# A hand-written order of work: its table of shifts and stretches with other numbers

## The reference

```
layer 0: qkvo = 1x1 conv(x); lepe = depthwise 5x5 conv(v)        # 12 heads of 32
         out  = proj((softmax(q k^T) v + lepe) * o)
layer 1: four directions k of a selective scan over 1024 points, 16 states n:
         dt = softplus(w_dt x_dbl + bias); h = exp(dt A) h + (dt u) B;  y += h C
         then layernorm over channels and gelu
layer 2: every group of channels shifted, then a 5x5 blur (here two small matmuls)
layer 3: softmax attention over 1024 points (one head), squeeze-and-excite gate, proj, batchnorm
```

## Time and profile before

| | us |
|---|---|
| median of 3 runs (10136.06 to 10141.46) | 10141.37 |
| the profiled execution's own time | 10139.04 |
| its span, first to last instruction | 10137.2 |
| DVE busy | 8021.4 (79%) |
| PE busy | 7191.2 (71%) |
| POOL busy | 4780.9 (47%) |
| ACT busy | 4127.9 (41%) |

### The profile page before, as it was taken

One profiled execution on the slowest core, in us unless ns is written; L12 is line 12 of the kernel. 1 busy time (PEld: TensorE's weight loads), 2 busy tenths in 40 slices (PEclk: granted clock), 3 DMA queues, 4 the chain that ended last, 5 costly groups with the idle time before them and its releaser, 6 DMA issues.

```text
span 10137.2 us, 100789 instructions
## 1 busy us (share of the span) xinstructions
PE 7191.2 (71%) x33528; PEld 3720.1 (37%) x33528; DVE 8021.4 (79%) x5358; ACT 4127.9 (41%) x4330; POOL 4780.9 (47%) x1990
## 2 busy tenths in 40 slices
PE   6746776777758777587776877767776777767556
PEld 2233334433334333443334433344333433344433
DVE  5477888778986898868987689877889678987992
ACT  3333443344433444334443344433443334433431
POOL 2155555345543454535644455444545345554660
PEclk9857886888769878697787878877887888778658
DMA  0165457645575445744567445665547644575782
GB/s 27 42 215 178 163 172 256 204 151 174 185 256 187 155 167 198 259 159 163 169 213 236 171 164 170 241 203 174 171 162 256 198 167 167 185 245 207 254 269 69
DMA packets 717956, 1875.92 MB, mean 185 GB/s; under 512 B 258896, under 2 KB 274640, under 8 KB 717264
## 3 DMA queue, kind: packets, MB, share of 16 engines
q1 hardware_dynamic: 717392, 1869.00, 54.4%
HBM read 1772.03 MB, written 71.04 MB: 182 GB/s over the span
## 4 chain that ended last, share of the span: by engine, by line
PE 38%; DVE 31%; issue 16%; ACT 6%; DMA 3%; DVEq 2%; SPq 2%; POOL 1%; ACTq 1%; POOLq 0%
DVE R L1771 14%; PE ps L977 8%; DVE ps L1761 7%; PE ps L843 7%; PE ps L1074 5%; DVE nmx L1691 4%; ACT R L1277 3%; PE ps L1162 3%; PE ps L986 2%; PE ps L957 2%; PE ps L991 2%; PE ps L1057 2%; PE ps L1145 2%; PE ps L1047 1%; PE ps L1131 1%
## 5 line engine op out<-in xcount | busy, mean ns | idle before, releaser
L1457 POOL TENSOR_TENSOR R<-R 128x1024 f32<-128x1024 f32 x1536 | 3688.6, 2402 | 4095.4 <-DVE ps L1761 3888.8
L1771 DVE TENSOR_TENSOR_SCAN R<-R,ps 128x1024 f32<-128x1024 f32 x1536 | 3507.4, 2283 | 350.7 <-ACT R L1335 237.1
L1335 ACT ACTIVATE R<-R,negA 128x1024 f32<-128x1024 f32 x1536 | 1748.8, 1143 | 2210.1 <-DVE R L1771 2177.9
L1074 PE MATMUL ps<-ident,R 128*128 128x128 f32 x12288 | 2162.5, 338 | 587.5 <-POOL R L1457 550.0
L1074 PEld LDWEIGHTS ps<-ident,R 128*128 128x128 f32 x12288 | 1820.8, 176 | 1566.7 <-issue 805.9
L1761 DVE TENSOR_TENSOR ps<-R 128x1024 f32<-128x1024 f32 x1536 | 2009.1, 1308 | 259.3 <-DMA R<-bc_scratch 147.2
L1277 ACT ACTIVATE R<-ps 128x1024 f32<-128x1024 f32 x768 | 786.3, 1024 | 1056.2 <-PE ps L977 1054.2
L957 PE MATMUL ps<-R 32*128 32x512 f32 x3072 | 668.6, 955 | 661.8 <-DVE nmx L1691 560.0
L977 PE MATMUL ps<-R 64*128 64x512 f32 x3072 | 914.0, 674 | 203.3 <-ACT R L1277 92.7
L1691 DVE TENSOR_REDUCE nmx<-ps 128x4 f32<-128x2048 f32 x384 | 872.3, 2280 | 184.8 <-PE ps L957 183.7
L843 PE MATMUL ps<-R 128*128 128x512 f32 (+1 forms) x1824 | 845.6, 620 | 175.3 <-DVE R L1629 96.9
(11 more groups left out here) (160 smaller groups left out, 5407.5 us busy)
## 6 DMA issues: line engine op xcount, KB each, us to landing
R<-bc_scratch SPq DMA_DIRECT2D x3072, 512.0 KB, 4.6
R<-in_x SPq DMA_DIRECT2D x72, 512.0 KB, 7.0
out<-R SPq DMA_DIRECT2D x72, 512.0 KB, 6.1
R<-shift_scratch SPq DMA_DIRECT2D x48, 640.0 KB, 7.0
R<-R SPq DMA_DIRECT2D x192, 128.0 KB
R<-out SPq DMA_DIRECT2D x48, 512.0 KB, 9.6
R<-in_w_qkvo SPq DMA_DIRECT2D x32, 576.0 KB, 10.1
rows_scratch<-R SPq DMA_DIRECT2D x24, 512.0 KB, 4.5
```

The lines of the kernel that those rows point to most:

```text
L1074: mm = pe.matmul(ps[:, 4 + b // 4, (b % 4) * P:(b % 4 + 1) * P], state[i % HELD][:, b * P:(b + 1) * P], ident[:, :], start=fresh and i % G ...
L1335: act.activation(decay[i % len(decay)], dt[:, c, :], ACT.Exp, scale=negA[:, col:col + 1]).then_inc(a_sb.h, 1)
L1457: pool.tensor_tensor(state[i % HELD], state[i % HELD], rows_c[slot], ALU.mult).then_inc(hc_sb.h, 1)
L1771: v.tensor_tensor_scan(h, a, b, 0.0, ALU.mult, ALU.add).then_inc(h_sb.h, 1)
```

## The change

Only numbers in the four tables change: 53 of 120 entries have other numbers, and eight entries are new (among them B, d and z of the scan). No event is added or removed, and no instruction changes.

```diff
 NORM_KINDS = ("ns", "nm", "nd", "nv", "ne", "nn")
 
 NORM_MOVED = {
-    ("nd", "attn0"): (-0.50, 1.00), ("nd", "attn3"): (0.79, 1.00), ("nd", "scan"): (2.93, 1.00),
-    ("ne", "attn3"): (-0.45, 0.88), ("ne", "blur"): (-0.01, 1.00), ("ne", "scan"): (3.43, 1.00),
-    ("nm", "attn0"): (-0.48, 1.00), ("nm", "attn3"): (0.11, 1.00), ("nm", "scan"): (2.68, 1.00),
+    ("nd", "attn0"): (-0.61, 1.00), ("nd", "attn3"): (0.79, 1.00), ("nd", "scan"): (2.73, 0.89),
+    ("ne", "attn3"): (-0.45, 0.88), ("ne", "blur"): (-0.01, 1.00), ("ne", "scan"): (3.01, 0.89),
+    ("nm", "attn0"): (-0.48, 1.00), ("nm", "attn3"): (0.11, 1.08), ("nm", "scan"): (2.62, 0.89),
     ("nn", "attn0"): (-0.50, 1.00), ("nn", "attn3"): (-1.16, 1.00), ("nn", "blur"): (-0.50, 1.00),
-    ("nn", "scan"): (3.19, 1.00), ("ns", "attn0"): (-0.50, 0.69), ("ns", "attn3"): (0.46, 1.00),
-    ("ns", "scan"): (3.18, 1.00), ("nv", "attn3"): (-0.10, 1.00), ("nv", "blur"): (0.14, 1.00),
-    ("nv", "scan"): (3.43, 1.00),
+    ("nn", "scan"): (2.68, 1.00), ("ns", "attn0"): (-0.50, 0.69), ("ns", "attn3"): (0.46, 1.00),
+    ("ns", "scan"): (4.02, 1.00), ("nv", "attn3"): (-0.10, 1.00), ("nv", "blur"): (-0.86, 1.00),
+    ("nv", "scan"): (3.12, 0.89),
 }
 LATE_MOVED = {
-    ("M2", 0): (-0.60, 0.82), ("O2", 0): (-0.64, 1.00), ("Q3", 0): (-0.73, 1.00), ("V3", 0): (-0.54, 0.92),
-    ("Y3", 0): (-0.90, 1.00), ("Y3", 1): (-0.61, 1.00), ("bl", 0): (-0.10, 1.20), ("cs", 0): (-0.18, 1.00),
-    ("e3", 0): (-0.10, 1.23), ("e3", 1): (-0.48, 1.03), ("f", 0): (0.76, 1.04), ("fx", 0): (1.47, 1.04),
-    ("gl", 0): (0.00, 0.67), ("k3", 0): (-0.10, 1.00), ("k3", 1): (-0.52, 1.03), ("ld2", 0): (-0.80, 1.01),
-    ("ldb", 0): (-0.10, 1.00), ("ln1", 0): (0.38, 1.07), ("m2", 0): (-0.50, 1.00), ("n3", 0): (-0.10, 1.00),
-    ("n3", 1): (-0.90, 1.03), ("o2", 0): (-0.60, 1.00), ("out", 0): (3.61, 1.00), ("p1", 0): (-0.88, 1.04),
-    ("p2", 0): (-0.96, 1.04), ("p3", 0): (-0.94, 1.04), ("p4", 0): (-1.45, 0.99), ("p5", 0): (-0.12, 1.04),
-    ("p6", 0): (1.02, 1.05), ("p7", 0): (-0.21, 1.04), ("park", 0): (-0.42, 1.00), ("q3", 0): (-0.25, 1.00),
-    ("r3", 0): (-0.10, 1.00), ("r3", 1): (-0.90, 1.28), ("s3", 0): (0.07, 1.00), ("s3", 1): (-0.90, 0.91),
-    ("sh", 0): (0.00, 0.99), ("st2", 0): (-0.50, 1.00), ("sto", 0): (-0.10, 1.05), ("t3", 0): (-0.10, 1.00),
-    ("t3", 1): (-0.48, 1.03), ("v3", 0): (-0.26, 1.00), ("w3a", 0): (-0.10, 1.00), ("w3b", 0): (-0.38, 1.10),
-    ("x3l", 0): (-0.95, 1.09), ("xc", 0): (0.00, 1.03), ("y3", 0): (-1.00, 1.00), ("y3", 1): (-0.61, 1.00),
+    ("M2", 0): (-0.60, 0.82), ("O2", 0): (-0.64, 1.00), ("Q3", 0): (-0.37, 1.00), ("V3", 0): (-0.55, 0.89),
+    ("Y3", 0): (-1.08, 1.00), ("Y3", 1): (-0.64, 1.00), ("bl", 0): (-0.10, 1.14), ("cs", 0): (-0.18, 1.00),
+    ("e3", 0): (-0.21, 1.19), ("e3", 1): (-0.51, 1.03), ("f", 0): (0.72, 1.04), ("fx", 0): (1.44, 1.04),
+    ("gl", 0): (0.85, 0.67), ("k3", 0): (-0.26, 0.97), ("k3", 1): (-0.55, 1.03), ("ld2", 0): (-0.80, 1.01),
+    ("ldb", 0): (-0.64, 1.00), ("ln1", 0): (0.38, 1.07), ("ln2", 0): (0.08, 1.00), ("m2", 0): (-0.50, 1.00),
+    ("n3", 0): (-0.39, 0.87), ("n3", 1): (-1.03, 1.03), ("o2", 0): (-0.60, 1.00), ("out", 0): (4.03, 1.00),
+    ("p1", 0): (-0.91, 1.04), ("p2", 0): (-0.99, 1.04), ("p3", 0): (-0.97, 1.04), ("p4", 0): (-0.39, 0.99),
+    ("p5", 0): (-0.16, 1.04), ("p6", 0): (1.23, 1.05), ("p7", 0): (-0.24, 1.04), ("park", 0): (-0.42, 1.00),
+    ("q3", 0): (-0.25, 1.00), ("r3", 0): (-0.20, 0.97), ("r3", 1): (-0.93, 1.28), ("s3", 0): (-0.03, 0.97),
+    ("s3", 1): (-1.03, 1.00), ("sh", 0): (0.00, 0.99), ("st2", 0): (-0.50, 1.00), ("sto", 0): (-0.10, 1.05),
+    ("t3", 0): (-0.24, 0.97), ("t3", 1): (-0.51, 1.03), ("v3", 0): (-0.26, 0.97), ("w3a", 0): (-0.10, 1.00),
+    ("w3b", 0): (-0.25, 0.99), ("x3l", 0): (-0.98, 1.09), ("xc", 0): (-0.89, 1.03), ("y3", 0): (-1.12, 1.00),
+    ("y3", 1): (-0.65, 1.00),
 }
 EARLY_MOVED = {
-    ("E", 2): (-0.52, 1.00), ("M", 1): (-0.07, 1.00), ("M", 2): (-0.30, 1.00), ("N", 1): (0.37, 0.91),
+    ("E", 2): (-0.52, 1.00), ("M", 1): (0.19, 1.00), ("M", 2): (-0.30, 1.00), ("N", 1): (0.37, 0.91),
     ("N", 2): (-0.02, 1.02), ("O", 1): (0.00, 0.97), ("O", 2): (0.35, 1.00), ("O", 3): (0.10, 1.00),
-    ("O", 4): (-0.42, 1.00), ("O", 5): (-0.42, 1.00), ("Qk", 0): (-0.13, 1.00), ("R", 0): (0.27, 1.00),
+    ("O", 4): (-0.42, 1.09), ("O", 5): (-0.42, 1.00), ("Qk", 0): (-0.13, 1.00), ("R", 0): (0.27, 1.00),
     ("R", 2): (0.35, 1.00), ("S", 0): (-0.10, 1.00), ("S", 2): (0.35, 1.00), ("T", 2): (-0.52, 1.00),
-    ("V", 2): (-0.42, 1.00), ("Vo", 0): (0.08, 1.00), ("Vt", 0): (-0.71, 1.00), ("Z", 2): (-0.42, 1.00),
-    ("dp", 0): (0.00, 0.90), ("dp", 2): (0.10, 1.00), ("dv", 0): (-0.01, 1.00), ("dv", 2): (-0.52, 0.86),
-    ("dw", 1): (-0.02, 1.02), ("dw", 2): (0.10, 1.00), ("mr", 2): (-0.52, 1.00), ("p0", 0): (0.18, 1.00),
-    ("pv", 0): (-0.10, 1.00), ("pv", 2): (0.10, 1.00), ("q2", 2): (0.10, 1.00), ("rg", 0): (0.18, 1.00),
+    ("V", 2): (-0.42, 1.00), ("Vo", 0): (0.08, 1.00), ("Vt", 0): (-0.71, 1.00), ("Z", 2): (-0.52, 1.00),
+    ("dp", 0): (0.00, 0.90), ("dp", 2): (0.20, 1.00), ("dv", 0): (-0.01, 1.00), ("dv", 1): (0.00, 1.02),
+    ("dv", 2): (-0.52, 0.86), ("dw", 1): (-0.02, 1.02), ("dw", 2): (0.10, 1.00), ("mr", 0): (-0.14, 1.14),
+    ("mr", 2): (-0.52, 1.00), ("p0", 0): (0.18, 1.00), ("pv", 0): (-0.10, 1.00), ("pv", 1): (0.03, 1.00),
+    ("pv", 2): (0.10, 1.00), ("q2", 2): (0.10, 1.00), ("qk", 0): (0.04, 1.00), ("rg", 0): (0.18, 1.00),
     ("tv", 0): (-0.60, 1.00), ("tv", 2): (0.10, 1.00), ("vo", 0): (-0.42, 1.00), ("vt", 0): (-0.60, 1.12),
-    ("vz", 0): (-1.03, 1.00), ("wg", 0): (-0.17, 1.00), ("x1", 0): (3.18, 1.00), ("x1s", 0): (3.18, 1.02),
-    ("xa", 0): (-2.17, 1.00), ("xb", 0): (-1.07, 0.96), ("xn", 0): (-0.42, 1.00), ("xr", 0): (-0.18, 1.00),
+    ("vz", 0): (-0.92, 1.00), ("wg", 0): (-0.17, 1.00), ("x1", 0): (3.18, 1.00), ("x1s", 0): (3.05, 0.90),
+    ("xa", 0): (-2.20, 1.00), ("xb", 0): (-1.07, 0.96), ("xn", 0): (-0.42, 1.00), ("xr", 0): (-0.18, 1.00),
 }
 SCAN_MOVED = {
-    ("C", 0): (-0.09, 1.00), ("K", 0): (0.10, 1.00), ("W", 0): (-1.14, 1.00), ("a", 0): (0.24, 1.00),
-    ("h", 0): (0.13, 1.00), ("l", 0): (-0.20, 1.00), ("t", 0): (-0.10, 1.00), ("x", 0): (-0.31, 1.00),
-    ("y", 0): (-0.32, 1.00),
+    ("B", 0): (-0.32, 1.00), ("C", 0): (-0.09, 1.00), ("K", 0): (0.10, 1.00), ("W", 0): (-1.09, 1.00),
+    ("a", 0): (0.28, 1.00), ("d", 0): (-1.07, 1.00), ("h", 0): (0.13, 1.00), ("l", 0): (-0.20, 1.00),
+    ("t", 0): (-0.10, 1.00), ("x", 0): (-0.31, 1.00), ("y", 0): (-0.32, 1.00), ("z", 0): (-0.01, 1.00),
 }
```

## The result

The changed kernel takes 10066.6 us (median of 4 runs, 10063.5 to 10067.9) against 10140.7: ratio 0.9929, 95% interval 0.9914 to 0.9944.

The account below looks back on a forecast made before the run. DVE, busy 8021.4 of 10137.2 us, was taken as the bound, its idle and stretched time the gain. Terms gave -6.0 us per loop pass, -8.3 first, +3.4 last, together -40.9: 10100 us, range 10072 to 10134.

Parts of the forecast that it names:

- The first term, vz: On DVE, s 64 in front of vz runs inside the wait for the last Vt: -2.2 us per loop pass.
- S34's: d3.0 and d3.1 one turn earlier around S32: R34's wait goes, R33's stays; -3.9 us per loop pass.
- the blur: d0.4 and d0.5 delay ACT, ldb 0 before C 25 gives back up to 1.3: +2.3 us at bl.
- The price of y3.5: d1.2 now stands before y3.5: +1.1 us at xa, and 1.1 in the last pass.
- The attention of layer 3: Held-up n3 against earlier s3.0 and s3.5: -0.1 us at r3.5, between -1.7 and +2.0.
- The norm: Scan's norm order: nn falls to 3.0 us for three, new wait about 2.1 before nd; -2.7 us per loop pass.
- d2.2 and d2.3: These two d one turn earlier in the scan: replayed with the trace's durations as 0.
- the slower rival: d ahead of decays on ACT costs 2.9 us at three more places: pass 2.7 us slower, 10160 us; chance 0.08.
- a new wait for L1335: Sign of a wrong prediction: DVE shows new waits for this line after the change.
- the last O: V47, d3.4, Z47: O waits 0.75 already and 1.12 are added, +1.1 us (0 to 2.1).
- that of R4 and R5: d1.4 and d1.5 earlier: R5's wait falls, R2 and R4 wait; -0.6 us, between -2 and +2.
- rival 3: Nothing held up behind b 39 and a short wait at nd: -1.6 and -1.2 more a pass, 10080 us; chance 0.11.

Follow-up runs that it names:

- d alone: The kernel before with only d of the scan one turn (1.07) earlier: 10133.7 us, ratio 0.9992.
- the old rows: The changed kernel with the rows B and ldb back at their old turns: 10087.4 us, ratio 0.9950.
- B alone: The kernel before with only the rows B 0.32 earlier, ldb at its old turn: 10130.9 us, ratio 0.9993.
- six-d kernel: The changed kernel with d earlier only for d1.4, d1.5, d2.4, d2.5, d3.0 and d3.1, the other 18 halves back: 10033.3 us, ratio 0.9896.
- vz and the norm alone: The kernel before with only vz behind s 64 and the six norm entries of scan as changed: 10092.6 us, ratio 0.9951.
- nd late: The kernel with d earlier for only eight halves, with nd of the scan's norm one event later, behind s 177: 10009.5 us, ratio 0.9877.
- both rows: The kernel before with only the rows B 0.32 and ldb 0.54 earlier: 10118.4 us, ratio 0.9979.
- ldb alone: The kernel before with only ldb 0.54 earlier: 10137.3 us, ratio 0.9997.

## Why the forecast was right in direction and too small

**What was right.** The first term, vz, was -2.2 and measured -2.3. S34's was -3.9, and R34's wait is gone as drawn (s 130: -5.1, with 1.2 that was not forecast at O3). The new wait at nd, forecast at 2.1, is 2.00, and nn at 3.0 is 3.02. The kind and size of the blur's cost to ACT was right: d alone brings the first sto 2.5 later against s 16 (38.8 us against 36.3), where 2.8 was forecast. The price of y3.5 (1.1) is +1.2 in the last pass.

**The step that failed: the blur.** The prediction said "ldb 0 in front of C 25 may give back up to 1.3", let B 25 count for nothing, and took +2.3 for this stretch. The cost itself was sized well (+2.7 with d alone, +2.5 with the old rows); the failed term is what the rows give back. The stretch measured -0.5, because the rows give back 3.2: 3.4 alone, 3.0 as the difference of the changed kernel and that with the old rows. The error was to price each turn on SP by itself. Singly each makes the stretch 1.2 shorter, little more than what is no effect; as a pair they shorten the way from sto to bl by 1.8, and the first sto itself comes 1.6 earlier (34.7 against 36.3; 34.9 with B alone). With 2.8 in seven passes this is 20 of the 31 us that the forecast lacked.

**The attention of layer 3.** Forecast -0.1, measured -2.2, and -4.6 in the last pass. The hold-up of n3 was bigger than assumed (three at 1.6 to 2.1 more each). But two terms on PE were too small: d1.0 and d1.1 (3.0 with the six-d kernel as base, given 0.7), and s3.5 in front of z 41 (2.0 in the third pass, given 0.9).

**The norm.** Forecast -2.7. nn ends 27.3 us after the start of s 175 instead of 30.8, in each of the six passes: -3.5, as ns itself no longer waits (0.42 before at L1612) and L1618, now L1620, is not held up (0.20). The whole stretch is 3.7 shorter, and 4.0 with vz and the norm alone, beside the lower bound of 3.9.

**Zeros that were not zero.** d2.2 and d2.3 were replayed as 0. S17 now stands behind d2.2 and ACT's two reads of it, and S18 behind d2.3: R17 waits 1.72 and R18 3.29. In the six-d kernel the same two:

```profile
4708.55 2.27 DVE L1694 TENSOR_REDUCE nmx<-ps 128x4 f32<-128x2048 f32 x1
...
4714.55 2.29 DVE L1694 TENSOR_REDUCE nmx<-ps 128x4 f32<-128x2048 f32 x1 [0.21 <-PE ps L960]
```

The stretch s 90 to 110 is 135.2 against 130.8 there. But R19 and R20, which waited 1.0 and 2.6 before, no longer wait, so from s 99 to s 103 the net cost is 1.8 of the 4.5. Some 1.5 more come in front of O at s 97 (a wait of 1.51), and 1.9 from s 107 to s 109, where neither PE nor ACT nor DVE has another order. Four d went back together in six d (d2.0 to d2.3), so it is not shown which of them these belong to. At s 150 the mechanism of the slower rival is seen: the decay is queued on ACT behind a d that waited for PE.

```profile
5049.35 0.69 ACT L1315 ACTIVATE R<-ps,vecs 128x512 f32<-128x512 f32 x1 [1.21 <-PE ps L1059]
...
5050.70 0.63 ACT L1319 ACTIVATE R<-R 128x512 f32<-128x512 f32 x1
5051.24 1.13 ACT L1337 ACTIVATE R<-R,negA 128x1024 f32<-128x1024 f32 x1
```

Measured from scan to scan as a mean of six passes, this costs 4.1 at s 150, of which shorter waits up to s 156 give back 2.7 (0.5 three times, and 1.3 in front of O). It is a new wait for L1335 (L1337 now), which the prediction had named as a sign of being wrong: the sign came, and yet the time was better than forecast. The gain of 3.0 at s 110 had been put at 0 as well. Against the forecast, the three zeros and the stretch of the last O (+3.6 for +1.1) are 5.3 too long, that of R4 and R5 (-2.1 for -0.6) and that of S34 2.7 too short. Of the +3.6 only the 1.1 in front of the last O was forecast; the rest are longer waits for ACT (L1294, 1.63 for 0.58) and for p0 on PE (L845, 2.70 for 1.00), which stay when d3.4 and d3.5 go back (1.30 and 2.70 in six d). These errors partly cancelled, which was luck; the replay was not good enough to call any of them 0.

**The first pass** gave 14.8 for 8.3. Parts do not add there: vz and norm alone give 13.5, d alone 8.1. What is known of it is below.

By the cases of the prediction this is rival 3, "more than forecast", but not by its mechanism, since n3 is held up and the 2.0 at nd is there.

## What to carry to other kernels

Price turns on a DMA queue as a queue, not one by one: replay all loads and stores between the two waits that a consumer sees, since a pair can be worth 21 us where one alone is worth 8 and the other 2, neither clear of nothing. Cut the time into numbered stretches and compare kernels with one part of a change each; a shift applied to all events of a kind (24 d here) is then seen to gain in some places and lose in others, and keeping it for eight of the 24 was worth another 56 us. An item put at zero by replay needs a bound from what is queued behind it, here two reads on ACT and the decay. And take a reading of a wait as a mean of all passes: with nd late, the loads seemed to take 1.5 us longer in the third pass alone, and PE was the cause in five of six.

## What the runs showed of the hardware

The same PE work can run at either clock. In the first pass of the kernel before and of that with vz and norm, PE's order is the same here, with the same waits of 0.54 (0.53) and 1.12 in front, 5 us apart. Timeline of PE before, then of vz and norm:

```profile
1425.88 1.13 PE L977 MATMUL ps<-R 64*128 64x512 f32 x4 [0.54 <-ACT R L1277]
1428.13 1.98 PE L1057 MATMUL ps<-R,w_dt 12*128 12x512 f32 x2 [1.12 <-ACT R L1277]
1430.04 1.93 PE L991 MATMUL ps<-R,ones 128*32 128x512 f32 x8
```

```profile
1420.92 1.13 PE L977 MATMUL ps<-R 64*128 64x512 f32 x4 [0.53 <-ACT R L1277]
1423.17 1.12 PE L1057 MATMUL ps<-R,w_dt 12*128 12x512 f32 x2 [1.12 <-ACT R L1277]
1424.22 1.07 PE L991 MATMUL ps<-R,ones 128*32 128x512 f32 x8
```

And the stretches of 5 us around them; the seventh figure is the granted clock (0.50 is 1.2 GHz, 1.00 is 2.4):

```profile
1425.00:1430.00 5.00, 3.34 (x10) 0.71 (x6) 4.80 (x3) 1.85 (x2) 1.69 (x2) 0.83 0.45 172
1430.00:1435.00 5.00, 5.00 (x21) 2.27 (x20) 1.69 (x2) 2.94 (x4) 2.23 (x1) 0.50 0.51 193
```

```profile
1420.00:1425.00 5.00, 3.34 (x18) 0.75 (x14) 4.76 (x3) 2.50 (x4) 1.87 (x2) 1.00 0.51 182
1425.00:1430.00 5.00, 4.87 (x32) 1.77 (x32) 2.45 (x3) 4.83 (x7) 2.27 (x1) 1.00 0.57 182
```

The clock falls behind the same idle time in one and stays up in the other, and the stretch s 146 to 160 takes 88.6 against 85.2 us. PE's waits in the 10 us before are the same too; those 18 to 25 us back are not (4.84 and 2.72 against 3.89 and 3.06). No order was touched in this stretch, so the difference comes from how far the passes were moved, by 5 us here, or from the execution itself: runs of the kernel before, all of one order, lie between 10126.4 and 10153.5 us. First passes with the order of before took 1086.3, 1086.3, 1085.9 and 1082.5 us (before, both rows, B alone, ldb alone); this much, up to 4 us, is no effect of a change. What decides between the two was not tried.

A row's b can be stretched as well: b 25, started early by the B row, takes 3.10 us in the changed kernel beside an h (POOL, 4195.78 for 2.35), and 3.29 with both rows, instead of 1.23. In both kernels it ends 1.1 us after the h. There the earlier row takes 2.7 off its wait (3.29 before, 0.63 now) and loses 2.1 of it at once.
